# Five products of a zeroed tile ahead of the first projection in a two-branch cross-attention kernel

## The reference, cut to what matters

```python
q = split_heads(x @ w_q)                       # x: (2, 2048, 640), 20 heads of 32
k, v = split_heads(text @ w_k), split_heads(text @ w_v)          # 69 text tokens
out_text = softmax(q k^T / sqrt(32)) v
k_ip, v_ip = split_heads(ip @ w_k_ip), split_heads(ip @ w_v_ip)  # 4 + 4 image tokens
mask_ip = _ip_mask(bbox, ...)                  # 0 or -10000 per query and box
out_ip = softmax(q k_ip^T / sqrt(32) + mask_ip) v_ip
out = (out_text + out_ip) @ w_out + b_out + x
```

## Time and profile before

| | us |
|---|---|
| median of 3 executions | 442.64 |
| lowest and highest of them | 442.2, 443.42 |
| the profiled execution, its own time | 441.82 |
| its span, first to last instruction | 440.0 |
| TensorE busy in the span | 422.5 |
| VectorE, GpSimd, ScalarE busy | 353.4, 157.0, 134.3 |
| mean granted clock of TensorE | 0.996 |

### The profile page before, as it was taken

One profiled execution on the slowest core, in us unless ns is written; L12 is line 12 of the kernel. 1 busy time (PEld: TensorE's weight loads), 2 busy tenths in 40 slices (PEclk: granted clock), 3 DMA queues, 4 the chain that ended last, 5 costly groups with the idle time before them and its releaser, 6 DMA issues.

```text
span 440.0 us, 17253 instructions
## 1 busy us (share of the span) xinstructions
PE 422.5 (96%) x7970; PEld 326.6 (74%) x7970; DVE 353.4 (80%) x466; ACT 134.3 (31%) x196; POOL 157.0 (36%) x129
## 2 busy tenths in 40 slices
PE   3789989989999999999999999999999999999996
PEld 3668868767777777777777777777777777777785
DVE  2386697799888998889888998899888988888712
ACT  4235534443323322243223323332224422222200
POOL 1164222368332642254233622255225422332200
PEclk9899999999999999999999999999999999999999
DMA  8969330014213312321115221331234111122333
GB/s 308 368 216 397 125 141 4 27 49 136 79 51 123 111 61 65 132 98 51 51 57 159 80 73 51 122 98 50 74 106 135 54 51 49 51 74 56 107 131 119
DMA packets 22391, 47.14 MB, mean 107 GB/s; under 512 B 2864, under 2 KB 2992, under 8 KB 22320
## 3 DMA queue, kind: packets, MB, share of 16 engines
q1 hardware_dynamic: 21744, 45.93, 30.4%
q10 hardware_dynamic: 576, 0.12, 0.1%
HBM read 35.55 MB, written 10.49 MB: 105 GB/s over the span
## 4 chain that ended last, share of the span: by engine, by line
PE 91%; DVE 4%; DMA 2%; ACT 1%; issue 1%; ACTq 0%
PE ps L580 65%; PE ps L632 13%; PE ps L613 8%; PE ps L660 3%; DMA bias<-in_b_out 2%; DVE scratch L524 1%; PE ps L666 1%; PE ps L704 1%; ACT vt L379 1%; DVE text_max L450 1%; DVE scratch L525 1%; DVE prob L456 1%; DVE den L474 0%; ACT prob L357 0%; DVE prob L467 0%
## 5 line engine op out<-in xcount | busy, mean ns | idle before, releaser
L321 POOL TENSOR_TENSOR prob<-prob,rden 128x1104 f32<-128x1104 f32 x40 | 82.3, 2059 | 233.2 <-DVE rden L479 233.2
L580 PE MATMUL ps<-x_hi,wq_hi 128*128 128x512 f32 x200 | 84.9, 425 | 2.6 <-DVE x_lo L537 2.6
L580 PE MATMUL ps<-o_hi,wo_hi 128*128 128x512 f32 x200 | 82.7, 413 | 0.0
L353 ACT ACTIVATE q<-ps 128x512 f32<-128x512 f32 x40 | 23.9, 597 | 190.9 <-PE ps L580 190.9
L580 PE MATMUL ps<-x_lo,wq_hi 128*128 128x512 f32 x200 | 79.2, 396 | 0.0
L580 PE MATMUL ps<-o_lo,wo_hi 128*128 128x512 f32 x200 | 79.1, 395 | 0.0
L580 PE MATMUL ps<-o_hi,wo_lo 128*128 128x512 f32 x200 | 79.0, 395 | 0.0
L580 PE MATMUL ps<-x_hi,wq_lo 128*128 128x512 f32 x200 | 79.0, 395 | 0.0
L486 DVE STREAM_TRANSPOSE prob_t<-prob 128x1536 f32<-128x1536 f32 x40 | 70.8, 1769 | 0.0
L450 DVE TENSOR_REDUCE text_max<-ps 128x16 f32<-128x1104 f32 x40 | 52.2, 1305 | 17.2 <-PE ps L613 13.0
L474 DVE TENSOR_REDUCE den<-prob 128x16 f32<-128x1104 f32 x40 | 52.0, 1299 | 14.4 <-ACT prob L357 14.4
(11 more groups left out here) (50 smaller groups left out, 397.6 us busy)
## 6 DMA issues: line engine op xcount, KB each, us to landing
stage<-in_x SPq DMA_DIRECT2D x38, 256.0 KB, 3.3
res<-in_x SPq DMA_DIRECT2D x37, 256.0 KB, 2.7
out_tiles<-res SPq DMA_DIRECT2D x37, 256.0 KB, 2.1
wk_raw<-in_w_k SPq DMA_DIRECT2D x5, 512.0 KB, 5.1
wki_raw<-in_w_k_ip SPq DMA_DIRECT2D x5, 512.0 KB, 7.4
wv_raw<-in_w_v SPq DMA_DIRECT2D x5, 512.0 KB, 6.7
wvi_raw<-in_w_v_ip SPq DMA_DIRECT2D x5, 512.0 KB, 7.5
stage<-in_w_q SPq DMA_DIRECT2D x5, 320.0 KB, 9.7
```

Source lines behind the costliest of these rows:

```text
L321: nc.gpsimd.tensor_tensor(e[:, :, 0:TEXT], e[:, :, 0:TEXT], rden[:, par, 0, :].unsqueeze(2).to_broadcast([P, QT * HG, TEXT]), ALU.mult)
L353: nc.scalar.activation(q[:, c % 2, :], ps[:, Q_BANK, :], ACT.Copy, scale=SCALE).then_inc(q_copied, 1)
L580: return nc.tensor.matmul(ps[:, bank, :], w[:, g, P * kt:P * kt + P], m[:, b, kt, :], start=(n == 0), stop=(n == 3 * KD - 1))
```

## The change

A new semaphore `zeros_set` and two names, `WARM_BANK` (7) and `WARM` (5). VectorE's first instruction now sets `q[:, 0, :]` (128 partitions by 512 float32) to zero. TensorE's first instructions now wait for this and multiply the first 128 columns of the tile by all 512, five times, in plain float32 into bank 7. Nothing reads the product. The wait for the context and `k_text(0)` stand behind it.

```diff
+        WARM_BANK, WARM = 7, 5
...
+        zeros_set = sem("zeros_set")
...
             def prologue():
+                nc.vector.memset(q[:, 0, :], 0.0).then_inc(zeros_set, 1)
                 nc.vector.memset(prob[:, :, :, TOKENS:KEYS], 0.0)
                 masks(0)
...
             def prologue():
+                pe.wait_ge(zeros_set, 1)
+                for n in range(WARM):
+                    nc.tensor.matmul(ps[:, WARM_BANK, :], q[:, 0, 0:P], q[:, 0, :], start=True, stop=True)
                 pe.wait_ge(ctx_loaded, 16)
                 k_text(0)
                 make_q(0, whole[0:12])
```

## The result

| | before | with the change |
|---|---|---|
| first series, median (executions) | 442.99 (6) | 445.03 (6), 443.04 to 445.66 |
| ratio, 95% interval | | 1.0043 (1.0028 to 1.0057) |
| profiled execution: time, span | 441.82, 440.0 | 444.79, 443.0 |
| mean granted clock | 0.996 | 0.992 |

The change made the kernel slower by 0.43%, outside the range on record. Two later series of the same kernel gave 0.9996 (0.9977 to 1.0015) and 1.0025 (1.0007 to 1.0042). They are part of what has to be explained, and stand with the experiments (runs 12 and 14). One execution of the kernel before, of 508.85 us at a granted clock of 0.76, is from a slow state of the chip and is counted nowhere.

The account below looks back on a forecast made before the run. TensorE's stream was taken to bound the kernel, its start waiting for the bias transfer through the masks. 441.82 us plus four zero terms gave 441.8; the forecast was set nearer the median, at 442.4 us, range 440.5 to 443.7 us.

Parts of the forecast that it names:

- What bounds the kernel: TensorE sets the end; at the start make_q(0) waits until 12.88 us for the bias transfer, masks and first x_lo.
- The five products: Start of TensorE: ten records, 0.455 us each at full clock or 0.853 at low, ending at 7.7 to 8.0 us.
- The clock at the start: Clock rises after 3.4 to 4.0 us of zero products, k_text(0) runs at full clock, the fall near 14 us stays.
- A: Start: clock rises during zero products, gap stays, clock falls in or soon after it; 441.8 to 443.2 us; chance 0.55.
- D: Clock falls inside the longer gap, so make_q(0) starts low; at most 1.0 us more, 443.6 us; chance 0.09.
- B: Clock does not fall behind the gap before make_q(0); worth 1.7 us, 440.9 or 440.1 us; chance 0.28.
- The sum: Whole kernel, profiled execution: 441.82 us plus four terms of 0, giving 441.8 us.
- Ten cost 4.6 us at full and 8.5 us at low clock: Start of TensorE: time of the ten records of the five zero products, scaled by columns from L660.
- Likeliest cost and likeliest gain: nothing: k_text(0) behind the zero products ends at about 9.9 us, while make_q(0) waits until 12.88 us anyway.
- Rival C: Start: zero products do not raise the clock, k_text(0) ends at 14.1 us; +2.2 us, 444.8 us; chance 0.08.
- chance of 0.13: Whole kernel slower by over 0.3%, above 444.0 us: 0.11 from C and a third of D, 0.02 for chance.
- H: Theory of the experiments: the zero products' work, or the clock they raise, has the slowing effect by itself.

Follow-up runs that it names:

- run 12: The change itself again, against the kernel before, beside the other runs: 442.87 us, ratio 0.9996.
- run 14: The change a third time, against the kernel before, as partner of the run with later token loads: 444.85 us, ratio 1.0025.
- run 9: Kernel before with VectorE's masks(0) behind the five x_lo instead of ahead of them: 438.82 us, ratio 0.9902.
- run 1: Kernel before with 21 more TensorE waits on the context's already set semaphore, no product added: 443.45 us, ratio 1.0008.
- run 4: Kernel before with only the zeroing of the tile on VectorE, no product and no wait: 443.41 us, ratio 1.0006.
- run 7: Kernel before with the first six products of make_q(8) moved ahead of make_scores(7): 442.29 us, ratio 0.9988.
- run 8: Changed kernel with the first six products of make_q(8) moved ahead of make_scores(7): 442.47 us, ratio 0.9986 to the kernel before.
- run 13: Changed kernel with SP holding step 5's three token loads until make_scores(7) is done: 443.18 us, ratio 0.9989 to the kernel before.
- run 10: Kernel before with masks(0) behind the five x_lo and six make_q(8) products ahead of make_scores(7): 438.41 us, ratio 0.9901.
- run 11: Changed kernel with masks(0) behind the five x_lo and six make_q(8) products ahead of make_scores(7): 437.95 us, ratio 0.9892 to the kernel before.
- run 15: Kernel before with masks behind the x_lo, six make_q(8) products ahead of make_scores(7) and later token loads: 438.28 us, ratio 0.9888.
- run 16: Changed kernel with masks behind the x_lo, six make_q(8) products ahead and later token loads: 439.06 us, ratio 0.9896 to the kernel before.
- run 5: Changed kernel with its five products cut to 32 by 32 columns, still ten pairs: 444.61 us, ratio 1.0034 to the kernel before.
- run 6: Changed kernel with two 512-column and 38 products of 32 by 32 in place of its five: 443.05 us, ratio 0.9996 to the kernel before.
- run 3: Kernel before with make_o(4) moved between the 9th and 10th product of make_q(7): 444.8 us, ratio 1.0038.

## Why the prediction was wrong

**What bounds the kernel, right.** The first projection waited for the bias transfer through the masks, not for TensorE. Run 9 shows it: taking the masks out of the way moved it from 12.88 to 10.56 us.

**The five products, nearly.** Ten records, 0.853 us apart at low clock, as scaled. They ended near 8.8 us where 7.7 to 8.0 was estimated, because the clock rose later. `k_text(0)` ended at 10.83 us, not 9.9. It cost nothing, since the slack reached to 12.88 us.

**The clock at the start, right in kind.** The clock fell again near 14 us in the profile of the first series (A). In those of runs 12 and 14 it fell inside the gap, so that the first projection was slow from its start (D, at 11.6 and 12.9 us); but so it was in runs 1, 4 and 7, without the change, whose clock rose only at 18.73, 19.15 and 18.10 us. B came in none of the five profiles that have the change's five products and the gap of the start (the first, runs 8, 12, 13 and 14). That the fall goes with the gap is shown by runs 9, 10, 11, 15 and 16: in none of these five profiles, with the masks moved and the gap at most 0.9 us long, does the clock fall near 14 us.

**The sum, wrong, by a term that it didn't have.** The failed step is "Ten cost 4.6 us at full and 8.5 us at low clock" together with "Likeliest cost and likeliest gain: nothing". The ten records were costed as time alone. They are also ten pairs of instructions ahead of a program whose code arrives in blocks, and the code 85 us later was moved against the blocks' edges by ten pairs. In the profiled execution this came to 2.71 us in that stretch, a term that stands at nothing in the sum: about 1.5 us for the hole and its edges and 1.2 us for the low clock. That the hole belongs to the place in the code is shown by the count of 3009. That the pairs and not the work make the whole kernel slower rests on runs 5 and 6: the ten pairs without the work are long in 8 of 12 executions, and the work with 80 pairs in none. Run 1 limits it: a shift that should have been enough gave 1 long execution of 12. Rival C did not come about, and D is not what separates the changed kernel from the one before; a slower kernel had its chance of 0.13 for reasons that were not the cause.

**What could have been seen in the trace before.** The row `PE ps L613 <- issue: 1.5` in the earlier trace rows was taken for a later wait and left unread. It marks the one place where 160 small products stand in a row around an idle stretch, with nothing large to cover a late block. In the trace before, the record behind the 3009th is the weight load of this product of `make_q(8)`:

```profile
95.64 0.51 PE L580 MATMUL ps<-x_lo,wq_hi 128*128 128x512 f32 x1
95.99 0.40 PE L580 MATMUL ps<-x_hi,wq_lo 128*128 128x512 f32 x1
```

It starts 2.3 us after the piece of 93.36 us went out, as behind the holes, and the next product comes 0.35 us later, not 0.23: the same lateness, covered by the large products.

**How large the effect is.** The three series of the change have 14 of 30 executions above 444.3 us, and a middle of 444.15 us; the kernel before has 0 of 6, 1 of 29, 1 of 34, 2 of 17 and 5 of 23. Part of an execution's time lies outside its span, and the spans alone tell the two apart better. Of the change, 15 of 30 are above 442.4 us; of the 103 executions of the kernel before whose spans are on record, none. Of those 15, 11 have a mean clock of 0.987 or 0.988; none of the 103 is below 0.991. So the change costs about 0 to 2 us, by which of its two groups an execution falls into, and 0.25% by the middle one of the three ratios. The first 1.0043 was at the upper end. That an execution above 444.3 us is one with the hole is inferred from the times; only the profiles show holes. Of the three of the change itself the first has it, run 12 has none, and run 14 has 0.2 us at that record. Run 14's profile, with a span of 441.7 us, was not one of the long executions.

**What stays open.** What makes a block late. The held-back loads speak for transfers in its way (1 of 12 against 7 of 12, and a new hole where the loads went), but one pair of runs does not settle it, and why the shares differ between series (5 of 6, 2 of 12, 7 of 12) was not found. Why the clock falls near 95 us in some executions was not found either. It fell there without a hole in the profiles of runs 3, 5, 6, 14 and 16, and did not in those of the kernel before and of runs 1, 4 and 12, which have the same wait of 1.46 us. H is ruled out for the hole, which runs 7 and 10 have without any zero product, but whether the zero products make this fall more frequent was not tested.

## What to carry to other kernels

Instructions added ahead of a long program may cost something even where their time is free: they move all later code against the edges of the blocks in which it is fetched, and a stretch of small products beside a wait may then run dry. When a small change at one end shows a loss at the other, count the records ahead of the new hole in several versions; the same count in all of them is the sign. And where an engine idles before its first large work, ask what it waits for before giving it something to do: moving the masks behind the first low parts was worth 1%, warming the clock nothing.

## What the hardware showed that was not expected

- Holes in TensorE's stream behind 3009 records in four versions (the change, runs 7, 8 and 10; 0.66 to 1.33 us) and behind 3265 in one (1.29 us), 256 apart. TensorE went on 2.2 to 2.4 us after the last 16 KB piece of the instruction queue had gone out.
- The clock column reads 1.00 ahead of the first change of level in a trace, whatever the level is: in the kernel before, `k_text(0)` took 4.02 us under a reading of 1.00, and 2.12 us at full clock.
- 80 pairs of 64-column float32 products with 128 columns of weights took 0.217 us each; 76 records of 32 by 32 took 3.03 us, 0.04 us each (run 6).
- The clock fell again behind a wait of 1.46 us among small products (runs 5 and 6), and did not in run 12 of the same length of wait.
